# A four-layer graph network on one core: relation products taken out of a table and put inside the gather round

## The reference

```python
def rgcn_conv(x, edge_index, edge_type, W, W_root, b):
    src, dst = (edge_index[0], edge_index[1])
    seg = dst * N_REL + edge_type
    x_src = x[src]
    summed = jax.ops.segment_sum(x_src, seg, num_segments=N_NODES * N_REL)
    cnt = jax.ops.segment_sum(jnp.ones((src.shape[0],), x.dtype), seg, num_segments=N_NODES * N_REL)
    agg = summed / jnp.maximum(cnt, 1.0)[:, None]
    agg = agg.reshape(N_NODES, N_REL, x.shape[1])
    return jnp.einsum('nrd,rdh->nh', agg, W) + x @ W_root + b

x = jax.nn.relu(rgcn_conv(x, edge_index, edge_type, W1, root1, b1))
x = rgcn_conv(x, edge_index, edge_type, W2, root2, b2)
```

## Time and profile before

| | us |
|---|---|
| median of 3 runs | 7771.3 |
| lowest, highest | 7764.43, 7775.73 |
| the profiled execution, its own time | 7765.49 |
| its span in the trace | 7763.7 |
| PE busy | 4088.5 (53%) |
| POOL busy | 4912.0 (63%) |
| DVE busy | 2131.0 (27%) |
| ACT busy | 2024.1 (26%) |
| mean granted clock of TensorE | 0.635 |

### The profile page before, as it was taken

The page is one execution under the profiler, slowest core; times in us unless marked ns, Lnnn a source line. Parts: engine busy times, 40 slices in busy tenths (PEclk is TensorE's granted clock), DMA queues, the critical chain, the costliest instruction groups (busy, mean ns, idle before and its releaser), DMA issues.

```text
span 7763.7 us, 97535 instructions
## 1 busy us (share of the span) xinstructions
PE 4088.5 (53%) x18001; PEld 3348.1 (43%) x18002; DVE 2131.0 (27%) x7521; ACT 2024.1 (26%) x5750; POOL 4912.0 (63%) x5278
## 2 busy tenths in 40 slices
PE   5756776693333365666666844333344444444443
PEld 3346666543333344555554433333333333344333
DVE  6743333332222235666653300000200000100001
ACT  1100000020000013444432243333333333333333
POOL 0057777617777737777750077777577777677776
PEclk9955555695655666666655766555565566666556
DMA  4412222161111113333320321112211111211112
GB/s 159 175 38 57 58 58 57 49 270 52 52 51 52 52 29 88 83 85 83 85 63 0 133 54 52 51 52 52 54 52 51 52 52 52 60 52 52 51 52 55
DMA packets 282560, 529.06 MB, mean 68 GB/s; under 512 B 120570, under 2 KB 165710, under 8 KB 269534
## 3 DMA queue, kind: packets, MB, share of 16 engines
q0 software_dynamic: 159744, 330.88, 16.8%
q1 hardware_dynamic: 117934, 193.34, 7.1%
q10 hardware_dynamic: 4656, 2.79, 0.1%
HBM read 377.76 MB, written 148.89 MB: 68 GB/s over the span
## 4 chain that ended last, share of the span: by engine, by line
POOL 47%; issue 27%; PE 15%; DVE 4%; DMA 3%; ACT 1%; DVEq 1%; POOLq 1%; SPq 0%; ACTq 0%
POOL GB L634 44%; PE PS L976 3%; PE PS L964 3%; PE PS L1076 2%; POOL H L634 2%; DMA GB<-table,IDX 2%; PE PS L1183 2%; PE PS L1027 1%; PE PS L1050 1%; DVE TOUT L1380 1%; DMA table<-TOUT 1%; PE PS L1044 1%; DVEq L459 1%; DVE TOUT L1626 0%; POOL H L681 0%
## 5 line engine op out<-in xcount | busy, mean ns | idle before, releaser
L634 POOL DMA_INDIRECT GB<-table,IDX x4160 | 3945.8, 949 | 1482.3 <-issue 1352.4
L976 PE MATMUL PS<-OH,GB 128*128 128x128 f32 x8320 | 1953.0, 428 | 2889.9 <-DMA GB<-table,IDX 2868.9
L976 PEld LDWEIGHTS PS<-OH,GB 128*128 128x128 f32 x8320 | 1802.0, 328 | 3041.6 <-issue 2663.4
L1400 DVE TENSOR_TENSOR ACC<-ACC,PS 128x128 f32 x666 | 190.0, 285 | 4336.7 <-PE PS L976 4332.7
L740 ACT COPY IDX<-idx 128x8 int32 x520 | 101.7, 196 | 2725.1 <-PE PS L976 2706.4
L729 ACT ACTIVATE OH<-iota_f,local 128x128 f32<-128x128 f32 x2496 | 761.8, 387 | 0.0
L628 POOL COPY STG<-X 128x128 f32 x150 | 48.5, 328 | 865.7 <-DVE X L1436 431.5
L634 POOL DMA_INDIRECT GB<-table_gat,IDX x416 | 421.2, 1012 | 127.6 <-issue 122.5
L634 POOL DMA_INDIRECT H<-table_gat,IDX x416 | 420.8, 1012 | 126.8 <-issue 125.6
L1183 PE MATMUL PS<-TOUT,OH 128*128 128x144 f32 x1664 | 427.3, 449 | 0.9 <-DVE TOUT L1626 0.9
L1183 PEld LDWEIGHTS PS<-TOUT,OH 128*128 128x128 f32 x1664 | 394.9, 330 | 2.5 <-issue 1.0
(11 more groups left out here) (271 smaller groups left out, 4117.6 us busy)
## 6 DMA issues: line engine op xcount, KB each, us to landing
table<-TOUT SPq DMA_DIRECT2D x100, 1024.0 KB, 3.9
GB<-table,IDX POOLq DMA_INDIRECT x4160, 2.5
TOUT<-local_row SPq DMA_DIRECT2D x104, 256.0 KB
table<-TOUT SPq DMA_DIRECT2D x50, 512.0 KB, 2.6
H<-etype_row SPq DMA_DIRECT2D x105, 64.0 KB
GB<-table_gat,IDX POOLq DMA_INDIRECT x416
H<-table_gat,IDX POOLq DMA_INDIRECT x416
table_gat<-TOUT SPq DMA_DIRECT2D x10, 340.0 KB, 2.7
```

Of the source, the lines that this page charges most:

```text
L634: pool.indirect_dma_start(out=out[:, j, :], out_offset=None, in_=r.table.dram[:, :], in_offset=bass.IndirectOffsetOnAxis(ap=idx[:, j:j + 1 ...
L976: return nc.tensor.matmul(PS[:, bank, 0:P], GB[:, b, j * r.width:j * r.width + P], oh(b, j), **at)
```

## The change

`table16` and its two making stages are gone. A convolution now sums raw source rows per node and type, and multiplies by the relation matrices inside the round:

- `near_round` replaces `r_l0a`, `r_l0b` and both tables; it runs twice, as `near_a` on the input `x` in DRAM and as `near_b` on `table1`, to which the relu's output is stored. The nodes of a tile are taken to lie within `NEAR` = 16; numbers 0 to 255 stand for (node, type). A tile that spans more goes to `wide`, tile by tile in eight parts.
- Per batch PE does 16 products of 128x128 (the sums of the last batch, one type after the other as weights, `NEARBY`, against `r.weights`), then eight products of 128x256 that collect this batch's rows by a one-hot of 256 columns (`HOT`) in four PSUM banks, then one product that places the last batch's 128 slots into its window of nodes.
- ACT copies the four banks to `NEARBY` with types outermost, copies the made block, and copies the indices four batches ahead. There are four row buffers (`ROWS`) instead of two.
- DVE makes the eight one-hots of 256 columns one batch ahead, one that places (`PLACED`), and adds one window. In `near_a` the one-hot is multiplied by a window of reciprocals of the counts that SP reads, broadcast to all partitions, from DRAM (`windows`, eight DMAs of 128 KB per batch); its sum per edge is kept in `wcol`, which `near_b` uses.
- The count runs by itself, ahead of `near_a`. Counts are transposed to 128 partitions (50 transposes), made reciprocal there (128x800) and written to `one_over` in DRAM.
- Root1's product with its bias is done up front and put in `sums`. Between the rounds are 49 transposes of `sums`, relu on ACT and DVE in 13 groups, 13 stores, root2's 13 products, and the additions of b2 and residual; `n_l0b` then only normalizes.
- In the tables of numbers, node numbers are clamped to the last node, so that the last batch of every round, the later layers' too, goes as one batch.
- `sums` and `aux` are no longer cleared by DVE (`aux` by POOL), the destinations are loaded first, a slow load of single numbers (`prev_last`) is gone, ACT takes the copies of `X` and of some columns, and the weight transposes of later layers come after the count.

The core of the diff (the wide path, the preparation of columns and declarations are left out):

SP:

```diff
-            store_table(t_l0a)
...
+            sp.wait_ge(degree, 3)
+            sp.dma_start(one_over.rearrange("(k p) r -> p k r", p=P), COUNTS.rearrange("p (k r) -> p k r", r=R16)).then_inc(over_out, 16)
+            sp.wait_ge(over_out, 16)
...
+            def windows(k, b, first):
+
+                if not first:
+                    sp.wait_ge(near_hot, k - 1)
+                bases = meta_of(sp, k, 4 + G, G)
+                for j in range(G):
+                    sp.dma_start(WINDOWS[b][:, j * RCOLS:(j + 1) * RCOLS],
+                                 one_over.rearrange("n r -> (n r)")[bass.ds(bases[j] * R16, RCOLS)].unsqueeze(0)
+                                 .to_broadcast([P, RCOLS])).then_inc(win_in[b], 16)
...
+            with sp.Fori(1, BATCHES // 2) as i:
+                for b in range(2):
+                    windows(2 * i + b, b, False)
+            sp.wait_ge(near_hot, BATCHES)
+            sp.dma_start(WR[:, 0:2048].rearrange("d (r h) -> d r h", r=R16),
+                         a["L0_gnn_W2"].rearrange("r d h -> d r h")).then_inc(w2_in, 16)
+            for g in range(GROUPS):
+                sp.wait_ge(h_made, g + 1)
+                sp.dma_start(table1[columns_of(g), :].rearrange("(n p) f -> p n f", p=P),
+                             h_rows(g).rearrange("p (n f) -> p n f", f=P)).then_inc(h_stored, 16)
```

POOL, and then ACT:

```diff
+            def gather_near(r):
+
+                with pool.Fori(0, BATCHES // FOUR) as i:
+                    for c in range(FOUR):
+                        k = FOUR * i + c
+                        pool.wait_ge(near_idx, k + (r.first + 1))
+                        pool.sem_inc(near_passed, 1)
+                        for j in range(G):
+                            pool.indirect_dma_start(
+                                out=ROWS[c][:, j * P:(j + 1) * P], out_offset=None, in_=r.dram[:, :],
+                                in_offset=bass.IndirectOffsetOnAxis(ap=IDX[:, c, j:j + 1], axis=0),
+                            ).then_inc(near_in[c], 16)
+
             pool.wait_ge(rows_out, 16 * (2 + 2 * HEADS))
-            gather(r_l0a)
-            stage_table(t_l0b, [sums])
-            gather(r_l0b)
+            pool.wait_ge(turn_ps, N_COLS + N_XG)
+            gather_near(near_a)
+            pool.wait_ge(h_stored, 16 * GROUPS)
+            pool.wait_ge(root_ps, GROUPS)
+            gather_near(near_b)
             stage_table(t_gat, [sums, aux[0:2 * HEADS, :], PEN])
...
+                    if 1 <= now <= BATCHES:
+                        act.wait_ge(made_ps, K)
+                        if now + here >= 3:
+                            act.wait_ge(placed, K - 2)
+                        act.copy(MADE[1 - b][:, :], PS[:, 4, 0:P]).then_inc(made_sb, 1)
+                    if now < BATCHES:
+                        if now + here >= 2:
+                            act.wait_ge(made_ps, K - 1)
+                        for n in range(r.UNITS):
+                            act.wait_ge(near_ps, K * r.UNITS + (n + 1))
+                            of, to = PS[:, n, :], NEARBY[b].rearrange("p (r s) -> p r s", r=R16)[:, :, n * 32:(n + 1) * 32]
+                            act.copy(to.rearrange("p r (j d) -> p r j d", j=2), of.rearrange("p (j d r) -> p r j d", j=2, d=NEAR))\
+                                .then_inc(near_sb, 1)
```

PE (what it drops, then the steady step, then what follows the first round):

```diff
-                            nc.tensor.matmul(PS[:, 4 + j % LOOKS, 0:P], ETR[:, b, j * P:(j + 1) * P],
-                                             aux[0:R16, bass.ds(bases[j], P)], start=True, stop=True).then_inc(look_ready, 1)
-
-                    sum_tiles(r_l0a, k, b, [(look_free, k * G + (LOOKS + G)), (r_l0a.gathered[b], (i + 1) * (16 * G))], look)
-            node_products(n_l0a, [(0, mat("L0_gnn_root1"), X)], [], [edges_done(r_l0a)])
-            multiply_table(t_l0b)
-            sum_round(r_l0b)
...
+                    if 1 <= now <= BATCHES:
+                        pe.wait_ge(near_sb, K * r.UNITS)
+                        if now + here >= 2:
+                            pe.wait_ge(made_sb, K - 1)
+                        for t in range(R16):
+                            ins = nc.tensor.matmul(PS[:, 4, 0:P], NEARBY[1 - b][:, t * P:(t + 1) * P],
+                                                   r.weights[:, t * P:(t + 1) * P], start=t == 0, stop=t == R16 - 1)
+                        ins.then_inc(made_ps, 1)
+                    if now < BATCHES:
+                        pe.wait_ge(near_in[c], i * (16 * G) + 16 * G * (r.first // FOUR + 1))
+                        pe.wait_ge(near_hot, K + 1)
+                        for n in range(r.UNITS):
+                            if now + here >= 1:
+                                pe.wait_ge(near_sb, (K - 1) * r.UNITS + (n + 1))
+                            for j in (2 * n, 2 * n + 1):
+                                ins = nc.tensor.matmul(PS[:, n, j % 2 * RCOLS:(j % 2 + 1) * RCOLS], ROWS[c][:, j * P:(j + 1) * P],
+                                                       HOT[b][:, j * RCOLS:(j + 1) * RCOLS], start=True, stop=True)
+                            ins.then_inc(near_ps, 1)
+                    if 1 <= now <= BATCHES:
+                        pe.wait_ge(made_sb, K)
+                        pe.wait_ge(place_hot, K)
+                        if now + here >= 2:
+                            pe.wait_ge(added, K - 1)
+                        nc.tensor.matmul(PS[:, 5, 0:P], MADE[1 - b][:, :], PLACED[1 - b][:, :], start=True, stop=True).then_inc(placed, 1)
...
+            near_round(near_a)
+            pe.wait_ge(added, BATCHES)
+            for g in range(GROUPS):
+                if g >= 4:
+                    pe.wait_ge(h_made, g - 3)
+                for n, q in enumerate(blocks_of(g)):
+                    ins = nc.tensor.transpose(PS[:, g % 4, n * P:(n + 1) * P], sums[:, q * P:(q + 1) * P], ident[:, :])
+                ins.then_inc(h_ps, 1)
+            for g in range(GROUPS):
+                pe.wait_ge(h_relu, g + 1)
+                if g >= 4:
+                    pe.wait_ge(root_sb, g - 3)
+                here = columns_of(g)
+                nc.tensor.matmul(PS[:, 4 + g % 4, 0:here.stop - here.start], mat("L0_gnn_root2"), H[:, here],
+                                 start=True, stop=True).then_inc(root_ps, 1)
+            pe.wait_ge(root_sb, GROUPS)
+            pe.wait_ge(h_made, GROUPS)
+            pe.wait_ge(w2_in, 16)
+            near_round(near_b)
+            pe.wait_ge(added, 2 * BATCHES)
+            node_products(n_l0b, [], layer_norm("sums", 0, None, 1, 1), [])
             multiply_table(t_gat)
```

DVE:

```diff
+                def hot(k, b, at_half):
+
+                    K = k + r.first
+                    if not isinstance(k, int) or K >= 2:
+                        dve.wait_ge(near_ps, (K - 1) * r.UNITS)
+                    if r.looks:
+                        dve.wait_ge(win_in[b], at_half * (16 * G))
                     for j in range(G):
+                        to, key = HOT[b][:, j * RCOLS:(j + 1) * RCOLS], key16[:, bass.ds(k * G + j, 1)]
+                        if r.looks:
+                            ins = dve.scalar_tensor_tensor(to, iota_w[:, :], key, WINDOWS[b][:, j * RCOLS:(j + 1) * RCOLS],
+                                                           ALU.is_equal, ALU.mult, accum_out=wstage[:, b, j:j + 1])
+                        else:
+                            ins = dve.tensor_scalar(to, iota_w[:, :], key, wcol[:, bass.ds(k * G + j, 1)], ALU.is_equal, ALU.mult)
+                    ins.then_inc(near_hot, 1)
...
+                    if now < BATCHES - 1:
+                        hot(k + 1, 1 - b, 2 * i + ((c + 1) // 2 + 1))
+                    if now < BATCHES:
+                        if now + here >= 2:
+                            dve.wait_ge(placed, K - 1)
+                        dve.tensor_scalar(PLACED[b], iota_f[:, :], place[:, bass.ds(k, 1)], None, ALU.is_equal).then_inc(place_hot, 1)
...
+                        dve.wait_ge(placed, K)
...
+                        dst = sums[:, bass.ds(base, P)]
+                        dve.tensor_tensor(dst, dst, PS[:, 5, 0:P], ALU.add).then_inc(added, 1)
...
+            near_round(near_a)
+            dve.wait_ge(added, BATCHES)
+            for g in range(GROUPS):
+                here = columns_of(g)
+                dve.tensor_scalar(H[:, here], sums[:, here], 0.0, None, ALU.max).then_inc(h_relu, 1)
...
+                here = columns_of(g)
+                dve.scalar_tensor_tensor(sums[:, here], PS[:, 4 + g % 4, 0:here.stop - here.start], vec("L0_gnn_b2"), X[:, here],
+                                         ALU.add, ALU.add).then_inc(root_sb, 1)
+            dve.wait_ge(root_sb, GROUPS)
+            dve.wait_ge(w_added, BATCHES)
+            dve.wait_ge(h_stored, 16 * GROUPS)
+            near_round(near_b)
```

(4 more changed lines are left out.)

672 lines of the change are left out of this document (418 added, 254 removed).

## The result

The changed kernel took 7345.69 us (median of 4 runs, 7340.86 to 7354.82), the kernel before 7767.86 beside it: a ratio of 0.9458, 95% interval 0.9442 to 0.9474, 422 us less. I had predicted 7345, in a range of 7250 to 7530. When most of the experiments ran, the kernel before took 9374 to 9470 us, the gather rounds being longer and the count and the norm not, so that such a run is compared only with runs of the same time and its trace is read inside a stage that kept its length.

A forecast was written before the change was run, and what follows sets the result against it. POOL's gathers were taken to bound the rounds, and PE with DVE the stretches between them. The terms -191 + 3 - 184 + 0 - 27 - 26 sum to -425 us from the median of 7771.3: forecast 7345 us, range 7250 to 7530.

The forecast's parts named there:

- between the rounds: Gap from round a's end to round b's first gather: 207 us falls to 23 (18 to 35), -184 us.
- the first collecting product: Sign that the prediction is right: the first product collecting rows in round a comes near 277 us.
- The start: Kernel start to round a's first product: 53 + 187 + 37 = 277 us instead of 468.2, -191 us.
- the count at 1.8 us per batch: Count running alone ahead of round a, at DVE's pace: 187 us, 156 to 213 by the ends 1.5 and 2.05.
- the degree part: Between count and round a: reciprocals on 128 partitions, transposes, DRAM write, windows read back, first one-hots: 37 us.
- Round a: First convolution's gather round: 10.54 us per batch (10.0 to 13.3), 1074 us instead of 1071, +3 us.
- Round b: Second convolution's gather round, first gather to first product behind it: POOL's price and the drain unchanged, 0 us.
- The norm: Norm of the first layer, behind round b: eight pairs at 6.7 us instead of 10.1, 54 us, -27 us.
- The last batches: Last batch of each of four later rounds, done in one go instead of tile by tile: 6.5 us each, -26.
- PE as the bound: Rival, both rounds: PE's clock falls in gaps, a step takes 12.6 us and POOL waits; 7816 us, chance 0.10.
- Weight loads: Rival, PE's step in both rounds: 25 loads not hidden behind products, 13.8 us per step; 8066 us, chance 0.03.
- POOL stretched by DVE: Rival, round a: DVE's one-hots lengthen gathers, 12.2 us per batch; 7520 us (7430 to 7640), chance 0.18.

The follow-up runs named there:

- count_pairs: The changed kernel with DVE reading flag and first node of two count batches at once instead of one: 9179.51 us, beside 9373.63 for the kernel before.
- norm_product: The changed kernel with two 128x400 products of no use per pair in the first layer's norm, where root2's had been: that stage 60.3 us instead of 72.6.

## Why the prediction was right or wrong

**The bound** was right: POOL's gathers set both rounds, and a table made at PE's pace was worth its whole time. The term that proved the largest, between the rounds, was 6 us off. Most of its pieces (49 transposes, relus behind them, the stores) had a row before; in the changed kernel the transposes take 5.6 us and root2's 13 products 10.7. That the total came within 1 us is luck: the first collecting product, which was to be the first sign, came at 331.6 us and not near 277.

**The start** was wrong by 54 us, all of it in one term, the count at 1.8 us per batch: 2.38 was outside both ends. I had taken two additions late in the old count for the new loop (2.05) and went below them because DVE's two one-hots need only 1.5. The step that failed is that those batches "read their numbers one batch at a time as the new loop does". They read one batch at a time, but stand behind the old loop, at addresses that are constants, and the trace has DVE's load of the numbers 0.29 us after the start of an addition there (386.53 after 386.24). In the new loop the address is worked out from the loop's counter, and every second load follows the jump back: it starts 1.10 us after the addition (202.59 after 201.49). count_pairs gives back 43 of the 60 us. The start of the count (49 for my 53) and the degree part (35 for 37) held.

**Round a** was wrong by 40 us in the good direction, and all of it is the pace: 10.54, taken from the attention round against POOL being slowed by DVE, was 10.1. The rest of the term held. POOL had gathered four batches during the count and issued the other 800 gathers from 339.6 to 1350.7 without a stop, so that there were 8 us to fill, 100 batches and 14 us to drain, where I had 18, 99 and 12; at the pace measured my form gives 1031 us for the 1033 that it took.

**Round b** took 8 us less, 10.06 per batch for 10.13.

**The norm** was wrong by 19 us at the step "the product with root2, the bias and the residual leave the pair's chain; I take 6.7": I took the work out and kept the clock that went with it, and the rest of the pair got slower at 0.58 instead of 0.77. norm_product shows that the chain can go at 7.4 us in the mean and 6.5 at best, at a clock of 0.89.

**The last batches** were priced from one drain in a conv round. The attention round's was 15, the others 5.9: 33 for my 26. The other 12 us are the variation of gathers from run to run.

**The rivals.** PE as the bound (0.10) did not come: its step at full clock is 7.97 us, and the clock of the rounds is 0.94 and 0.97. Weight loads (0.03): 16 loads of 3.65 us lie within 16 products of 3.84. By one rule of the Trainium skill, "TensorE: Matmul & The Clock Gate", section "The mechanism", a load overlaps a running product only where the row group differs, and such loads would not; the same section also lets a load into the background weight buffer be pulled ahead. The step shows that they do overlap, or that their time is in the 1.88 ns per column in any case. POOL stretched by DVE (0.18) did not come either: what single gathers of round a lost to one-hots adds up to 12 us, as the last section shows.

## What to carry to other kernels

Price work that leaves an engine together with the clock that is left: where the granted clock of a stretch is between its levels, a product taken out can cost as much as it saves, and one of no use in a wait can pay. When a loop is taken apart, look at what shared a read, a wait or a pipeline fill in the old one; a few tenths of a us of register reads per batch were 43 us here. When the price of a loop is taken from rows that stand outside it, look whether its addresses are constants there. And compare a right total term by term before trusting the steps that led to it.

## What the runs showed that I had not expected

- Dense products of no use made a chain shorter: 60.3 and 61.4 us instead of 70 to 76 for the first norm, and 34.0 instead of 37.4 per pair in the second.
- What a DVE operation costs a gather depends on when in it the gather starts. In the changed kernel one that fell on a one-hot of the count, three of round a, and one of round b:

```profile
58.46 1.22 DVE L1688 TENSOR_TENSOR OH<-iota_w,local 128x1024 bf16<-128x1024 f32 x1
58.63 1.87 POOL L734 DMA_INDIRECT GB<-in_x,IDX  x1 [0.30 <-issue]
```
```profile
343.23 0.48 DVE L1723 SCALAR_TENSOR_TENSOR OH<-iota_w,key,H 128x256 f32<-128x256 f32 x1 [4.18 <-DMA H<-one_over]
343.33 1.20 POOL L734 DMA_INDIRECT GB<-in_x,IDX  x1 [0.30 <-issue]
...
344.45 0.48 DVE L1723 SCALAR_TENSOR_TENSOR OH<-iota_w,key,H 128x256 f32<-128x256 f32 x1
344.83 0.94 POOL L734 DMA_INDIRECT GB<-in_x,IDX  x1 [0.30 <-issue]
...
346.08 0.94 POOL L734 DMA_INDIRECT GB<-in_x,IDX  x1 [0.31 <-issue]
```
```profile
2264.12 2.35 DVE L1726 TENSOR_SCALAR OH<-iota_w,key,wcol 128x256 f32<-128x256 f32 x7 [1.09 <-DVEq L1791]
2264.58 1.10 POOL L734 DMA_INDIRECT H<-table,IDX  x1 [0.30 <-issue]
```

  The first starts 0.17 us into the one-hot and takes 1.87 us, 0.93 more than alone, which is about what the one-hot has left. The one at 343.33 starts 0.10 us into a one-hot of 0.48 and takes 0.26 more; the one at 344.83 starts 0.38 into one and loses nothing, nor does the one at 346.08, which starts together with one. So it goes all through round a. Of its 800 gathers behind the first 32, 58 started between 0.10 and 0.30 us into a one-hot, and each of them took 1.01 to 1.20 us, the longer the earlier it started; the 520 that started beside none took 0.945 in the mean and at most 0.962. All together this is 12 us in round a, and 6 in round b, whose one-hots take 0.41 us instead of 0.44 to 0.48 and whose longest gather has 1.10. The Trainium skill, "SBUF — State Buffer", section "SBUF: two separate sides", has an exclusive lock, held for the whole of an operation, for DVE operations with two SBUF inputs against GpSimd operations that read SBUF. The first row and the one at 343.33 are as it says; the ends of round a's one-hots are freer than that. Round b's one-hots read one SBUF tensor and two columns, and hold gathers up too; whether they fall under the section's other form, a mode that takes two ports, no run here shows.
